# Self attentions of a four-layer decoder: where ScalarE evicts value rows and features within a half batch

## What is computed

```python
q, k, v = heads(x @ Wq.T), heads(x @ Wk.T), heads(x @ Wv.T)   # 16 heads of 8
scores = einsum('bhqd,bhkd->bhqk', q, k) * SCALE              # causal, but for layer 2
attn = softmax(scores)
out = einsum('bhqk,bhkd->bhqd', attn, v)
x = x + out.reshape(B, T, D) @ Wo.T
```

## Time and profile before

| | |
|---|---|
| median of 3 runs | 6444.49 us |
| the three runs | 6421.35, 6444.49, 6450.44 us |
| the profiled execution, its own time | 6416.58 us |
| span of the profiled execution | 6414.8 us |
| PE busy, share of the span | 4773.7 us, 74% |
| DVE busy | 3437.4 us, 54% |
| ACT busy | 2451.0 us, 38% |
| POOL busy | 1999.7 us, 31% |
| mean granted clock of TensorE | 0.768 |

### The profile page before, as it was taken

One profiled execution on the slowest core, in us unless ns is written; L12 is line 12 of the kernel. 1 busy time (PEld: TensorE's weight loads), 2 busy tenths in 40 slices (PEclk: granted clock), 3 DMA queues, 4 the chain that ended last, 5 costly groups with the idle time before them and its releaser, 6 DMA issues. The chain is left out here.

```text
span 6414.8 us, 80803 instructions
## 1 busy us (share of the span) xinstructions
PE 4773.7 (74%) x20662; PEld 3396.3 (53%) x20662; DVE 3437.4 (54%) x5067; ACT 2451.0 (38%) x3674; POOL 1999.7 (31%) x1091
## 2 busy tenths in 40 slices
PE   7889999999797876667768888888467344432598
PEld 5768888888543765346655555555256122221344
DVE  3344444444344322444446666664633999996444
ACT  2245555555222211123325555555122555550122
POOL 0045555555100001000016666665000455550000
PEclk6579999999798556765559999998655666665699
DMA  2100000000011212120112111120020000000011
GB/s 72 46 8 15 15 15 15 15 15 8 19 43 51 37 28 62 43 79 20 32 27 45 44 42 41 41 47 21 3 50 16 17 21 24 25 15 0 0 46 40
DMA packets 153360, 193.03 MB, mean 30 GB/s; under 512 B 91760, under 2 KB 136576, under 8 KB 152864
## 3 DMA queue, kind: packets, MB, share of 16 engines
q1 hardware_dynamic: 152992, 188.87, 12.1%
HBM read 134.07 MB, written 19.05 MB: 24 GB/s over the span
## 5 line engine op out<-in xcount | busy, mean ns | idle before, releaser
L1021 POOL TENSOR_TENSOR pexp_lo<-arena,pexp_hi 128x800 fp32r<-128x800 f32 x384 | 727.8, 1895 | 423.9 <-POOLq L1020 423.4
L976 POOL TENSOR_TENSOR pexp_lo<-arena,pexp_hi 128x800 fp32r<-128x800 f32 x384 | 628.4, 1637 | 504.4 <-POOLq L975 504.4
L1940 DVE TENSOR_REDUCE arena<-ps 128x1 f32<-128x482 f32 (+3 forms) x624 | 393.3, 657 | 397.3 <-DVEq L1918 382.8
L2085 DVE TENSOR_REDUCE arena<-ps 100x1 f32<-100x482 f32 (+1 forms) x768 | 477.0, 656 | 222.1 <-DVEq L2054 204.3
L1275 ACT ACTIVATE arena<-ps 128x800 f32<-128x800 f32 x384 | 322.3, 839 | 545.5 <-ACTq L1273 543.5
L1341 ACT ACTIVATE arena<-ps 128x800 f32<-128x800 f32 x384 | 321.7, 838 | 407.9 <-ACTq L1335 402.6
L2655 PEld LDWEIGHTS ps<-arena 100*100 100x100 f32 x2560 | 455.0, 283 | 17.2 <-issue 4.1
L1725 DVE TENSOR_REDUCE arena<-ps 100x8 f32<-100x800 f32 x160 | 158.7, 992 | 541.9 <-DVEq L1722 541.9
L2655 PE MATMUL ps<-arena 100*100 100x9 f32 (+1 forms) x2560 | 428.8, 312 | 2.7 <-PEq L2647 2.7
L2392 DVE MATCH_REPLACE8 arena<-arena 100x1444 f32<-100x1444 f32 x256 | 430.1, 1728 | 0.0
L3009 PE MATMUL ps<-kst,qs 96*100 96x482 f32 (+1 forms) x768 | 334.6, 437 | 116.5 <-PEq L2969 112.5
(11 more groups left out here) (356 smaller groups left out, 10539.2 us busy)
## 6 DMA issues: line engine op xcount, KB each, us to landing
ctxT<-in_ctxT SPq DMA_DIRECT2D x64, 541.5 KB
ctxk<-in_ctx SPq DMA_DIRECT2D x48, 528.0 KB
kst<-mid SPq DMA_DIRECT2D x128, 180.5 KB, 3.1
heads_dram<-arena SPq DMA_DIRECT2D x20, 800.0 KB
chunk<-in_ff_chunks SPq DMA_DIRECT2D x77, 193.0 KB, 2.4
arena<-gate_dram SPq DMA_DIRECT2D x64, 200.0 KB, 3.1
kst<-xn SPq DMA_DIRECT2D x64, 180.5 KB, 2.9
q_rows<-heads_dram SPq DMA_DIRECT2D x36, 200.0 KB
```

The costliest lines, as they stand in the source:

```text
L976: own(nc.gpsimd.tensor_tensor(pexp_lo[p % 3][:, :, :], pexp[p % 3], pexp_hi[p % 3][:, :, :], ALU.subtract))
L1021: own(nc.gpsimd.tensor_tensor(pexp2_lo[p % 3][:, :, :], pexp2[p % 3], pexp2_hi[p % 3][:, :, :], ALU.subtract))
L1940: peak = nc.vector.tensor_reduce(mparts[0:at.stop - at.start, m, c:c + 1], bank(k, z - a, at.stop - at.start), AX.X, ALU.max)
L2085: peak = nc.vector.tensor_reduce(mparts2[:, h, c:c + 1], bank(k, z - a, S), AX.X, ALU.max)
```

## The change

Only ACT's stream is edited. The side jobs of half batch k move behind the exponential of half batch k + 1, ahead of its two copies; `root()` moves from the end of half batch 2 to just behind its exponential. No instruction is added or taken away, and the streams of PE, DVE, POOL and SP are as before. Across the border of two units `sides(7, ...)` is called, which has no job, as 7 stands in neither table.

```diff
+            def sides(k, u, par, first, last):
+
+                if k in VALUES_AT[nsm] and not last:
+                    i = VALUES_AT[nsm].index(k)
+                    value_rows(1 - par, i, 4 * (u + 1) + i if cfg.get("gate") else None)
+                if not first and k in TURNS_AT[nsm]:
+                    features(k - TURNS_AT[nsm][0])
+
             def unit(u, par, first=False, last=False):
                 for k in range(8):
                     act.wait_ge(s.shifted, 1)
...
                                          scale=float(cfg["scale"])).then_inc(s.probs_ready, 1)
+                    if not first and k == 2 and cfg.get("diff"):
+                        root()
+                    if k > 0:
+                        sides(k - 1, u, par, first, last)
+                    elif not first:
+                        sides(7, u - 1, 1 - par, u == 1, False)
                     for c in range(2):
                         act.wait_ge(s.turned, 1)
                         act.sem_inc(s.turned, -1)
                         nc.scalar.activation(probsT[:, k % 2, c * GT:c * GT + GT], bank(4 + c, GT, S),
                                              ACT.Copy).then_inc(s.probsT_ready, 1)
-                    if k in VALUES_AT[nsm] and not last:
-                        i = VALUES_AT[nsm].index(k)
-                        value_rows(1 - par, i, 4 * (u + 1) + i if cfg.get("gate") else None)
-                    if not first and k == 2 and cfg.get("diff"):
-                        root()
-                    if not first and k in TURNS_AT[nsm]:
-                        features(k - TURNS_AT[nsm][0])
```

## The result

The changed kernel takes 6239.93 us in the median of 4 runs (6222.43 to 6243.46), the kernel before 6432.92 in 4 (6412.84 to 6450.44). The ratio is 0.9696, 95% interval 0.9657 to 0.9734. It is faster by 193 us where 174.7 were worked out, and lies within the stated range.

What follows compares the result with a forecast made beforehand. PE bounds plain half batches; at a side job the round PE, ACT's eviction, ACT's exponential, PE does. 87.4 + 55.5 + 31.8 = 174.7 us off 6433.2 gave 6258 us, range 6229 to 6282.

Steps and rivals of the forecast that it cites:

- The plain pieces: PE's idle time ahead of its transposes at side jobs, all four stages: goes whole, 87.4 + 55.5 us.
- The eviction ahead of the copies: ACT's side eviction before the next half batch's copies: copy not late, by 0.1 to 0.2 us; costed at nothing.
- The square root: Earlier root in sa2: 4.8 us saved in each of six units, 3.0 in the last, together 31.8 us.
- The table load: Load ahead of sa2's square root, now behind an exponential: nothing extra taken; 5.8 or about 10 us if it drained.
- Rival A: In sa2 the square root's gain is not recovered, only 142.9 us go: 6290 us; 7 in 100.
- Rival B: TensorE's clock rises in the four loops as PE becomes busy throughout: some 340 us more, 5918; 4 in 100.
- Rival C: PE waits at proj_free for bank 6 inside the loops: stages 52 us longer, 6485; 3 in 100.
- Rival D: Something hidden in the earlier trace puts the idle pieces back: time stays near 6433 us; 3 in 100.
- The level: Starting time of the kernel before: mean of four known executions, 6433.2 us, between 6416.6 and 6450.4.

Runs made afterwards that it cites:

- e4: Against the changed kernel, features and square root back at their old places, only the value rows moved: 6302.75 us, 0.9788 of the kernel before.
- e5: Against the changed kernel, side evictions put behind the copies of the next half batch as well: 6229.78 us, 0.9660 of the kernel before.
- e6: Against the changed kernel, side evictions put one half batch later: 6230.94 us, 0.9679 of the kernel before.
- e2: Against the changed kernel, square root back at its old place behind the copies: 6258.70 us, 0.9708 of the kernel before.
- e3: Against the kernel before, only the square root moved behind its exponential: 6420.51 us, 0.9962 of the kernel before.
- e1: The changed kernel run again without an edit: 6228.31 us, 0.9672 of the kernel before.
- e7: Against the changed kernel, DVE's shift of half batch 3 put ahead of its wait for the square root: 6216.18 us, 0.9650 of the kernel before.

## Why the prediction was right, point by point

- **The plain pieces.** Right: the wait went in full, all 45 pieces of sa0, sa1 and sa3 and the 28 of sa2 (e4: 96.0 us for the 50 value rows, and the remaining pieces counted exactly). Mis-sized by 0.21 us each, 15 us in all: I took the drawn idle time for the cost of the piece, where the plain half batch of the earlier trace rows already showed a turn starting without any. The cost of a wait is turn to turn with it (8.70 us in sa0 by the turns at 102.49 and 111.19 of before) less turn to turn without it (6.53 now): 2.17 and not 1.96. For the same reason turn to turn over a value row came out at 6.53 us in sa0 and 5.52 in sa2, where 6.7 and 5.7 were said.
- **The eviction ahead of the copies.** Right: costed at nothing, and the first copy starts 1.03 us after the turn, 0.03 late. e5 and e6 show how much room there is.
- **The square root.** Right to a tenth of a microsecond: 1.6 us per unit and 3.4 in the last were said to stay, 1.62 (1.99 once) and 3.42 were found, 13.5 to 13.9 us in all. In the last unit the 0.25 us of latency, an estimate without a row behind it, came out so: the sum ends at 3103.73 and the load starts at 3103.98. e2 gives it 32.1 us of waiting, e3 only 17.9 when it moves alone, so it was also right to work it out on the schedule that the first move makes, and not as a separate item.
- **The table load.** The value taken, nothing extra, was right: the load starts 0.02 us behind an 800-column exponential. The drain of which the Trainium skill's page "ScalarE: Activation LUTs" tells, section "What ACT_TABLE_LOAD costs", does not show here either; its 1283 ns for the load do.
- **Rival A** was wrong by e2 against e1. **Rival B**: the loops' granted clock stayed low, 17 to 38 us of some 850 at 2.4 GHz against 14 to 21 of 1050 before; a fully busy PE did not raise it, as the earlier trace rows said. In e7 it was busy for 316.1 of the 317.2 us of sa2's loop, with no burst at all. The bursts at the beginning of sa1, and in three traces of sa2, came only with the value rows moved: a small piece of rival B. **Rival C**: no wait at L2615, L2672 or L2682 inside the loops of the changed kernel; e6 had to put the eviction a half batch later to see the first 0.33 us. **Rival D** fell with the result.
- **The level.** I took the mean of four known executions, 6433.2, for the kernel before; 17 runs gave 6442.1 and 11 gave 6433.85. The forecast of 6258 is 18 us over the first median and 30 over the second. Of this 15 are the overlap, some 5 to 11 the additional bursts, and the rest lies in the scatter outside the loops, where one stretch alone is 25 us long or short.

## What to carry to other kernels

Where an engine serves two chains in one loop, put first what the bound engine waits for next, here the exponential, and let the chores whose inputs come later stand behind it: their order costs nothing as long as each chore is done before its buffer is asked for again, and that slack can be read from the timeline. Work out a wait's cost from start to start of the bound engine's steps, with and without it, and not from the idle time alone. And compare the edited stretches first: two spans of one profile each can agree with a forecast by errors that cancel.

## What the runs showed of the hardware

- TensorE stays at 1.2 GHz (granted 0.50) in loops in which it is busy without a gap, in small float32 matmuls. The bursts at 2.4 GHz start 1.4 to 2.8 us behind the end of a project's matmuls (44 of 54, all 17 of those in kernels whose value rows are not moved); in six of the seven traces with the value rows moved there is also one of 10.2 us, 4 us behind the first turn of sa1, over half batches whose value rows now follow without a gap. A window inside it (columns as in the earlier trace rows):

```profile
2073.00:2082.00 9.00, 8.25 (x85) 7.78 (x83) 6.49 (x9) 4.81 (x10) 0.00 (x0) 1.00 0.01 3
```

  PE is busy 8.25 of 9 us in it, with 85 matmuls; in the earlier trace rows it was busy 4.00 of 4.00 with 24 and was not granted the higher clock. In three traces (changed, e2, e5) one of 6.8 us stands at the same place in sa2. Why the clock rises there and not at the beginning of sa0 and sa3 is open; no run was made on it.

- The unedited stretch between sa1 and sa2 takes 549 to 553 or 575 to 577 us, with the granted clock at 0.70 to 0.71 or 0.65 to 0.66, in kernels with and without the change. A profile each of two kernels can therefore differ by 25 us in a place that no one touched.
